# Loading the first head group's stack straight from the terms' buffer, with later projections in the prologue and the value bias folded once

## The reference

```
x = x + 0.5 * ffn(layernorm(x))                       # 8 experts, capacity limit per expert
q, k, v = layernorm(x) @ Wq.T + bq, ... @ Wkv.T + bkv # 16 heads of 16
dots = (q * 16**-0.5) @ k.T, masked above the diagonal
x = x + softmax(dots) @ v @ Wo.T + bo
x = x + 0.5 * ffn(layernorm(x))
# in ffn: keep = counts <= cap; an expert chosen more often than cap has all its tokens dropped
```

## Time and profile before

| | us |
|---|---|
| median of 3 runs (1365.21 to 1366.24) | 1365.62 |
| the profiled execution | 1366.13 |
| its span, first to last instruction | 1364.3 |
| first score matmul of maxima (PE, L1321) | 32.73 |
| first score matmul of batch 0 (PE, L1306) | 76.48 |

### The profile page before, as it was taken

The page is one execution under the profiler, slowest core; times in us unless marked ns, Lnnn a source line. Parts: engine busy times, 40 slices in busy tenths (PEclk is TensorE's granted clock), DMA queues, the critical chain, the costliest instruction groups (busy, mean ns, idle before and its releaser), DMA issues.

```text
span 1364.3 us, 25092 instructions
## 1 busy us (share of the span) xinstructions
PE 1257.0 (92%) x8697; PEld 600.3 (44%) x8697; DVE 1092.6 (80%) x3521; ACT 940.5 (69%) x1697; POOL 397.8 (29%) x508
## 2 busy tenths in 40 slices
PE   7789999999999999999999999999999999999874
PEld 5333344444454444454444444544445544444332
DVE  5798888778887888878887788878888788789744
ACT  2257776777767777767777777677777677776752
POOL 4323332322232322332323333323222323222111
PEclk9989999999999999999999999999999999999887
DMA  5770333542325444334435433254342143330001
GB/s 143 137 126 13 71 70 59 101 91 57 69 39 101 90 70 71 60 65 89 70 59 101 71 75 69 40 101 90 70 71 55 33 96 71 59 71 31 1 1 34
DMA packets 57832, 95.18 MB, mean 70 GB/s; under 512 B 8352, under 2 KB 51488, under 8 KB 51744
## 3 DMA queue, kind: packets, MB, share of 16 engines
q1 hardware_dynamic: 54800, 91.52, 35.8%
q10 hardware_dynamic: 2896, 1.98, 0.6%
HBM read 59.91 MB, written 33.55 MB: 69 GB/s over the span
## 4 chain that ended last, share of the span: by engine, by line
PE 60%; DVE 23%; ACT 7%; issue 4%; DVEq 3%; POOL 2%; DMA 1%; SPq 1%; ACTq 0%; POOLq 0%
PE o_bank L1340 15%; PE s L1321 13%; PE st L1306 12%; DVE s L1027 10%; PE misc L1222 6%; PE misc L1206 4%; PE misc L1214 4%; DVE max_full L1031 3%; ACT probs L867 3%; PE misc L547 3%; DVEq L1040 2%; ACT q_stack L854 2%; DVE xn L523 1%; DMA part_dram<-parts 1%; DVE stats L514 1%
## 5 line engine op out<-in xcount | busy, mean ns | idle before, releaser
L867 ACT ACTIVATE probs<-st 128x512 f32<-128x512 f32 (+1 forms) x1216 | 632.8, 582 | 191.0 <-PE st L1306 120.9
L1027 DVE CUSTOM_DVE_ANT_0 s<-s,causal 128x128 f32<-128x128 f32 (+3 forms) x1024 | 496.4, 506 | 118.2 <-PE s L1321 113.3
L1321 PE MATMUL s<-k_stack,q_stack 96*128 96x512 bf16 (+3 forms) x1536 | 494.9, 332 | 36.3 <-DVE max_diag L1027 17.9
L1306 PE MATMUL st<-q_stack,k_stack 108*128 108x512 bf16 (+3 forms) x1536 | 484.9, 328 | 12.8 <-ACT probs L867 12.2
L1031 DVE TENSOR_REDUCE max_full<-s 128x1 f32<-128x512 f32 x512 | 349.8, 683 | 44.0 <-PE s L1321 44.0
L1340 PE MATMUL o_bank<-probs,v_aug 128*17 128x512 f32 (+3 forms) x3072 | 324.9, 495 | 5.5 <-POOL probs L739 5.3
L1321 PEld LDWEIGHTS s<-k_stack,q_stack 96*128 96x128 bf16 x1536 | 149.5, 98 | 369.5 <-DVE max_diag L1027 161.2
L739 POOL TENSOR_SCALAR_AFFINE_SELECT probs<-probs 128x512 f32<-128x512 f32 x256 | 162.8, 636 | 468.3 <-ACT probs L867 467.9
L1306 PEld LDWEIGHTS st<-q_stack,k_stack 108*128 108x128 bf16 x1536 | 150.5, 98 | 98.3 <-ACT probs L867 37.4
L751 POOL TENSOR_TENSOR qk<-qk,parts 128x512 f32<-128x512 f32 x64 | 74.5, 1164 | 280.5 <-ACT parts L827 280.5
L1027 DVE DVE_READ_ACCUMULATOR2_ANT max_diag<- 128x1 f32 x1024 | 144.0, 141 | 0.1
(11 more groups left out here) (113 smaller groups left out, 886.0 us busy)
## 6 DMA issues: line engine op xcount, KB each, us to landing
part_dram<-parts SPq DMA_DIRECT2D x128, 192.0 KB, 2.8
k_stack<-part_dram SPq DMA_DIRECT2D x186, 128.0 KB, 7.3
q_stack<-part_dram SPq DMA_DIRECT2D x31, 384.0 KB, 4.9
x_all<-x SPq DMA_DIRECT2D x16, 512.0 KB, 11.5
q_stack<-part_dram SPq DMA_DIRECT2D x31, 256.0 KB, 7.4
out<-x_all SPq DMA_DIRECT2D x7, 1024.0 KB, 11.2
q_stack<-part_dram SPq DMA_DIRECT2D x31, 128.0 KB, 8.9
k_stack<-part_dram SPq DMA_DIRECT2D x12, 64.0 KB, 4.2
```

The source lines that it names most:

```text
L867: nc.scalar.activation(probs[:, g % 2, h - part:h + 1, 0:width], st_bank[i % 3][:, 0:share * width] .rearrange("p (h c) -> p h c", c=width ...
L1027: nc.vector.tensor_tensor_reduce(out=bank, in0=bank, in1=causal[:, CW - width:CW], scale=1.0, scalar=-BIG, op0=ALU.add, op1=ALU.max, accum ...
L1306: score = nc.tensor.matmul(st_bank[i % 3][:, part * width:(part + 1) * width], k_stack[0:KROWS + MROWS, hg, h, jb * P:(jb + 1) * P], q_sta ...
L1321: nc.tensor.matmul(s_bank[u % 3][:, 0:width], q_stack[0:KROWS, hm, h, ib * P:(ib + 1) * P], k_stack[0:KROWS, hm, h, j0:j0 + width], start= ...
```

## The change

It does four things.

1. **Group 0 is loaded from `parts` directly.** SP no longer writes its halves to `part_dram`; it copies six k blocks and one q block from `parts` into the stacks, and ACT (`qload`) copies the five other q blocks. All 12 copies of a half have 16 partitions x 4 x 512 (64 KB). They count up `first_half_in` and `second_half_in` (new). ACT's evictions of (1,0) and (1,1), which overwrite `parts`, wait for these. `qload` 0 moves ahead of the value evictions.
2. **The constant key rows** of groups 1, 2, 3 are written at other places: group 1 before the first `q2`, group 2 where 1 was, group 3 after the second `q2`.
3. **The projections (2,0) to (3,1)** stand six units later.
4. **The value bias** is multiplied by `w_o` once (two matmuls into all 128 rows), and added to `bo_row` by POOL. `ont` becomes one plain copy of 512 columns.

```diff
-    "pro_qk": (10, 20, 29, 38, 47),
+    "pro_qk": (10, 26, 35, 44, 53),
...
-    plan = [(3, "warm", WARM[0])] + ones(0) + norm(0) + turn(0) + norm(1) + [(3, "weights",)] + project(0, 0) + turn(1)
-    plan += ones(1) + project(0, 1) + ones(2, 3) + [(3, "use", "v", j) for j in range(2)] + [(3, "qload", 0)]
-    plan += [(3, "use", "v", j) for j in range(2, 4)] + [(3, "use", "qk", 1, 0), (3, "qload", 1), (3, "warm", WARM[1])]
+    plan = [(3, "warm", WARM[0])] + ones(0) + norm(0) + turn(0) + norm(1) + [(3, "weights",)] + ones(1) + project(0, 0) + turn(1)
+    plan += ones(2) + project(0, 1) + [(3, "qload", 0)] + ones(3) + [(3, "use", "v", j) for j in range(2)]
+    plan += [(3, "use", "v", j) for j in range(2, 4)]
+    if spec:
+        plan += [(3, "use", "bias")]
+    plan += [(3, "use", "qk", 1, 0), (3, "qload", 1), (3, "warm", WARM[1])]
...
+                    if b < 0 and hq == 0:
+                        landed, cols = (sig.first_half_in, sig.second_half_in)[c], slice(c * CW, (c + 1) * CW)
+                        for r, times, part in RUNS:
+                            for copy in range(times):
+                                rows = slice((r + copy) * HD, (r + copy + 1) * HD)
+                                eng.dma_start(k_stack[rows, 0, :, cols], parts[HG * HD:, c, part, :])\
+                                   .then_inc(landed, 16)
+                        eng.dma_start(q_stack[rows, 0, :, cols], parts[0:HG * HD, c, 0, :]).then_inc(landed, 16)
+                        return
+                    if b < 0 and hq == 1:
+                        eng.wait_ge((sig.first_half_in, sig.second_half_in)[c], HALF_IN)
+                        eng.sem_inc(sig.parts_out[c], 32)
...
-                    wait(eng, sig.parts_out[c], lin(b, 32 * NG, 32 * m))
+                    if b < 0 and hq == 1:
+                        eng.wait_ge((sig.first_half_in, sig.second_half_in)[c], HALF_IN)
+                    else:
+                        wait(eng, sig.parts_out[c], lin(b, 32 * NG, 32 * m))
...
+                elif kind == "use" and a[0] == "bias":
+                    eng.wait_ge(sig.misc_free, n("use", 2))
+                    nc.gpsimd.tensor_tensor(bo_row[:, 0, :], bo_row[:, 0, :], xg_t[:, 0, 0:D], ALU.add)
...
-                    for dc in range(DC):
-                        last = nc.scalar.activation(o_t[:, dc, :], bank[:, dc * 2 * P:(dc + 1) * 2 * P],
-                                                    ACT.Identity, bias=v_bias[:, dc:dc + 1])
-                    last.then_inc(sig.misc_free, 1)
+                    nc.scalar.activation(o_t[:, :, :], pair_view(bank), ACT.Copy).then_inc(sig.misc_free, 1)
...
+                elif what == "bias":
+                    for dc in range(DC):
+                        last = nc.tensor.matmul(bank[:, 0:D], v_bias[:, dc:dc + 1].to_broadcast([P, P]), w_o[:, dc, :],
+                                                start=dc == 0, stop=dc == DC - 1)
```

45 lines of the change are left out of this document (20 added, 25 removed).

## The result

| | before | after |
|---|---|---|
| median, us | 1365.21 (5 runs, 1364.72 to 1366.24) | 1358.59 (5 runs, 1357.43 to 1360.15) |
| the profiled execution, and its span | 1366.13, 1364.3 | 1358.59, 1356.8 |
| first projection on PE | 14.41 | 13.96 |
| unit 0 | 32.73 | 33.13 |
| first score matmul of batch 0 | 76.48 | 71.31 |

The ratio is 0.9947, with a 95% interval of 0.9935 to 0.9960: the changed kernel is faster by 5.5 to 8.9 us, 7.2 in the middle; the two medians in the table are 6.6 apart. 1358.9 was predicted.

What follows compares the result with a forecast made beforehand. The prediction named a prologue hole, ACT's eviction of (3,0) waiting for a DRAM write queued behind group 1's loads. Prologue 4.8 plus outputs 1.9 gave 6.7 us: 1359.4 profiled, median 1358.9, range 1354.8 to 1363.1.

Steps and rivals of the forecast that it cites:

- Unit 0 at 33.59: Start of units on PE: the bias's two fp32 matmuls cost 0.86 us, moving unit 0 from 32.73.
- ACT's copies, and the lag of 0.8: Prologue: ACT's copies at 0.71 to 0.93 us each and PE's delay shift all that follows by 0.8, range 0.5 to 2.2.
- Landing taken as 4.4: Group 0's copies within the chip: 4.4 us to landing, taken from loads of the same shape; range 3.0 to 7.
- Unit 44 at 58.4: Prologue on DVE: unit 44 starts at its old 57.60 plus 0.8 and ends at 59.1.
- The write of (2,0) lands at 62.6: DMA queue: old landing 62.19 plus 0.8, less 0 to 1.3 us for 384 KB less in the queue.
- Group 1's loads land ahead of unit 48: Prologue: group 1's loads land at 61.5, and unit 48 is wanted at 62.3.
- The CAST at 65.4 with 2.3 us of wait: DVE, behind unit 50: the CAST starts at 65.4, and 2.3 us of the 6.75 us wait stay.
- From unit 51 to 60 at the full clock 4.6, at the half level 5.59: Units behind the hole: 4.6 us at full clock gains 5.35, 5.59 at half level gains 4.4; 4.8 taken.
- (3,1) just in time, first score at 71 to 72: End of prologue: projection (3,1) ready at 69.7 for 69.8; batch 0's first score at 71 to 72 instead of 76.48.
- The prologue's term: Gain from the shorter hole ahead of batch 0: 4.8 us, bounds 2.5 to 6.5.
- The outputs, 8 x 0.24 = 1.9: Output evictions: 0.24 us saved on each of eight on the path, six in the body, two in the end.
- The rival of the dear copies: On-chip copies ending later than 48 turn the result slower; at 20 us to landing, 1373; slower 0.06.

Runs made afterwards that it cites:

- warm4: Changed kernel with 4 instead of 20 warm matmuls ahead of unit 0; median 1357.89 us, ratio 0.9934 to the kernel before.
- all_three: Changed kernel with group 1's stack loaded by halves, the bias's product in unit 16 and 4 warm matmuls; median 1357.54 us, 0.9935 of the kernel before.
- clock_kept: Changed kernel with three warm matmuls instead of one in each of units 14 to 19; median 1359.21 us, ratio 0.9947 to the kernel before.
- bias_late: Changed kernel with the bias's two matmuls in unit 16 and POOL's add in unit 21; median 1359.97 us, ratio 0.9951 to the kernel before.
- two_copies: Changed kernel with each output eviction again two copies of 256 columns, without a bias; median 1360.43 us, ratio 0.9954 to the kernel before.
- bias_alone: Kernel before with only the folded value bias and one 512-column output copy; median 1364.05 us, ratio 0.9984 to the kernel before.
- places_alone: Kernel before with only the later units 26, 35, 44, 53 for projections (2,0) to (3,1); median 1359.42 us, ratio 0.9958.
- direct_old_places: Changed kernel with projections (2,0) to (3,1) back at units 20, 29, 38, 47; median 1364.43 us, ratio 0.9985 to the kernel before.
- half_clock_warm4: Changed kernel with group 1's half loads, three warm matmuls in units 14-19 and 46-49, 4 ahead of unit 0; 1354.96 us, 0.9921 of before.
- half_old_places: Changed kernel with group 1's stack loaded by halves and projections (2,0) to (3,1) at their old units; median 1362.15 us, 0.9967 of before.
- half_loads: Changed kernel with group 1's stack loaded in halves, after the writes of (1,0) and (1,1); median 1358.50 us, 0.9938 of the kernel before.
- half_clock: Changed kernel with group 1's half loads and three warm matmuls in units 14 to 19 and 46 to 49; median 1356.64 us, 0.9936 of before.

## Why the prediction was right, point by point

The total was 0.3 us off, and the mechanism is the predicted one: the CAST moved behind unit 50. Some of its steps were wrong and made up for each other, so that the 0.3 is in part luck: the CAST came 1.1 us later than I had it, the clock behind it stayed up, which is worth 0.5 more than the middle that I took, and what lies behind the first score gave 0.4 more than the outputs' term. The prediction's times count from the start of before, so they are held against the common start.

- **Unit 0 at 33.59.** 33.58. Right, and for the stated reason: the bias costs 0.86 on PE, and no wait for `first_half_in` was seen.
- **ACT's copies, and the lag of 0.8.** Each copy takes 0.62 to 0.67 to issue, not 0.71 to 0.93. The step that failed is "evicts (1,0) and then issues five copies": the issue ran beside the evictions, ACT was free at 33.7 and not at 35.6 to 36.7, and the lag at unit 16 was 0.16. It does become the limit when unit 0 comes earlier (warm4, all_three).
- **Landing taken as 4.4.** 3.1 and 3.3, and 4.0 for SP's two of the q block. Neither eviction of group 1 waited for a copy. A landing on the chip is nearer to the write's 3.00 than to the load's 4.2; I had chosen the wrong neighbour.
- **Unit 44 at 58.4.** 59.37. The pace between 16 and 44 was taken from before, where nothing waits. Missing are 1.6 us, of which the fall of the clock at 44 us is 1.3 (what clock_kept won back); the lag was 0.6 too dear. Neither reached the end, since both lie in front of DVE's wait for the write.
- **The write of (2,0) lands at 62.6.** 63.7. That 384 KB less in the queue would give up to 1.3 us was wrong. From SP's first load of group 1 to ACT's eviction behind that write it took 13.5 us before, 13.7 after, and 13.5 to 14.5 in the seven other kernels with whole loads. In these kernels the landing followed the start of those loads, and they started 1.3 later than before, where I had 0.8. Of the 1.3, the write of (1,1) was issued 0.3 later (45.36 against 45.05), and took 4.7 us to the first load instead of 3.7.
- **Group 1's loads land ahead of unit 48.** Wrong: PE waited 2.2 us for them. It cost DVE nothing in the changed kernel: in its trace the last step of `mfin` starts at 62.64 and unit 48 on DVE at 62.75, with no wait. Where units come earlier, DVE waits there too, and its two waits together grow: 3.75 in clock_kept and 4.22 in bias_late, for 2.47. It is why earlier units alone give nothing.
- **The CAST at 65.4 with 2.3 us of wait.** 66.54 and 2.47.
- **From unit 51 to 60 at the full clock 4.6, at the half level 5.59.** 66.44 to 70.99 is 4.55, at a clock of 1.00, so the better of the two cases held and paid for most of the late CAST: unit 60 at 71.44 against 75.85. The Trainium skill (page "TensorE: Matmul & The Clock Gate", section "HAM oscillation — how this bites in real kernels") tells of waits for DMA of about 3 to 5 us behind which the work starts cold. I had held that against a silence of 2.3 us, which is shorter. The rows agree with the page on these waits: behind PE's wait of 2.2 us in the changed kernel the clock stayed at 1.00, behind those of 3.0, 4.1 and 4.7 us in warm4, clock_kept and bias_late it was 0.50. The fall near 44 us, with no idle time above 1.15 us ahead of it, is not of this kind.
- **(3,1) just in time, first score at 71 to 72.** 0.27 late before its CAST; first score at 71.76. The prologue's term was 4.8 and is 4.7.
- **The outputs, 8 x 0.24 = 1.9.** Behind the first score 2.3 us were gained, and the batches that are alike are 0.24 shorter, one eviction's worth each. The size was right, but three quarters of it come from the bias operand, as two_copies shows. The six in the body are what the wait list of the whole run has, before and after (shown below; with two plain copies the six waits are 3.0 us); the two at the end were not followed, and bias_alone has 3.6 us behind the first score where the changed kernel has 2.3.

```profile
PE misc L1222 <- ACT o_t L848: 4.1, 6, 0.7
...
PE misc L1235 <- ACT o_t L865: 2.6, 6, 0.4
```

- **The sum.** 4.7 + 2.3 + 0.45 of an earlier start in the profiled execution, 7.5 between the spans, for 6.7 predicted; the start is no gain of the change.
- **Which part carries it.** The prediction gave the hole to the shifted places, and rightly. The direct loads it had as neutral at unit 0 and as part of what frees the queue; they are worth nothing measurable here (0.9984 and 0.9985). With the later places, direct loads and bias together cost 1.2 us at the first score (70.57 against 71.76). That is not the bias's 0.86: of it 0.08 are left at unit 16 and 0.24 when the write of (1,1) is issued (45.12 against 45.36). The loads of group 1 then start 1.5 later (48.57 against 50.07), because that write took 3.5 us to the first of them in places_alone and 4.7 in the changed kernel, for the same bytes. Whether this belongs to the change or to the single execution is open: it took 3.5 to 3.9 in four of the nine kernels with whole loads (before, places_alone, direct_old_places, warm4) and 4.6 to 5.0 in the other five.
- **The rival of the dear copies** needed copies that end later than 48; ACT's last was issued by 33.3 and landed some 3.3 later. Of the port rule cited from the Trainium skill (page "SBUF — State Buffer", section "Door 1: The DMA port swizzle") no run shows a price: 64 KB into 16 partitions landed sooner from the chip than from DRAM.

What stays open: the intervals of most versions overlap, and these are told apart by their traces alone. Clear are these: half_clock_warm4 lies below places_alone, two_copies and bias_late; direct_old_places and bias_alone lie above all that have the later places; and half_old_places lies above warm4, half_loads, all_three, half_clock and half_clock_warm4. One or two of the batches are 0.8 to 2.6 us longer than 159.2 in most traces, at differing places; in two_copies the clock was down in that batch, and in eight others it read 1.00 throughout, so that the cause is open. Whether loads of group 1 straight from `parts` would beat half loads was not tried.

## What to carry to other kernels

When an engine stands before an instruction in its queue, there are two cures: move that instruction back in the queue, or let its input come sooner. The first was worth 5.7 us here; the second pays only if it reaches the transfer that was really late, which is found by measuring from the first transfer ahead of it in the queue and not from its own issue. Before starting something earlier, ask what it will run into: clock_kept and bias_late brought units forward by 1.3 and 2.2 us and gave nothing, and holding the clock up gave 0.9 at the first score once the loads in front of unit 48 were moved. And work moved out of a stretch in which TensorE has little to do can take the clock down there (1.12 busy of 2 us before, 0.65 after).
